# One set of work orders for another in a causal-attention kernel on one core, with two score banks and four transpose banks in PSUM where there were three and three

## What is computed (the reference, cut)

```python
h = layernorm(x) * (1 + ca) + sa                 # ca, sa, ga, ... come from silu(c) @ wmod, six sections
k, q, v = (einsum('ihd,bpd->biph', W, h) for W in (W_K, W_Q, W_V))
scores = einsum('biph,biqh->biqp', k, q)         # 2048 x 2048 for each head, causal mask
attn = softmax(masked / sqrt(128), axis=-1)
z = einsum('biqp,biph->biqh', attn, v)
x = x + ga * einsum('df,bqf->bqd', W_O, z_flat)
h = layernorm(x) * (1 + cb) + sb
w_gu, w_down = dequant_fp4(...)                  # packed 4-bit codes times group scales
y = einsum('bsi,hi->bsh', silu(gate) * up, w_down)   # gate, up = h @ w_gu
x = x + gb * y / rms(y)
```

## Time and profile before

| | us |
|---|---|
| three runs | 2268.33, 2266.88, 2264.04 (median 2266.88) |
| the profiled execution | 2263.7, with a span of 2261.9 |
| TensorE busy | 2124.0 of the span |
| VectorE, ScalarE, GpSimd busy | 1347.8, 1040.4, 714.0 |
| mean granted TensorE clock | 0.975 of full speed |

### The profile page before, as it was taken

How to read it: one execution, slowest core, us unless ns; L and a number is a source line. 1 busy time by engine, 2 the same in 40 slices (tenths; PEclk the granted TensorE clock), 3 DMA queues, 4 the chain that set the end, 5 groups by cost and what they waited for, 6 DMA issues and landing times. The chain is left out here.

```text
span 2261.9 us, 36789 instructions
## 1 busy us (share of the span) xinstructions
PE 2124.0 (94%) x12049; PEld 1831.7 (81%) x12049; DVE 1347.8 (60%) x3062; ACT 1040.4 (46%) x1947; POOL 714.0 (32%) x542
## 2 busy tenths in 40 slices
PE   6999798989989898999989899999999899999899
PEld 4778687978878797888879799999999788788687
DVE  7322365555646556565655656556556577799865
ACT  3322344544445454454545455555555333588611
POOL 4310233251523326143342600000005444388400
PEclk8999999999999999999999999999999999999999
DMA  7576302122120311212021120210223666211111
GB/s 251 175 206 190 109 27 87 32 67 63 39 70 26 86 42 60 63 35 72 23 86 49 49 63 11 63 56 12 60 63 100 211 233 200 106 59 38 52 65 65
DMA packets 171419, 189.99 MB, mean 84 GB/s; under 512 B 13395, under 2 KB 119123, under 8 KB 171219
## 3 DMA queue, kind: packets, MB, share of 16 engines
q1 hardware_dynamic: 169043, 184.89, 26.4%
q10 hardware_dynamic: 2304, 4.20, 0.5%
HBM read 121.53 MB, written 67.50 MB: 84 GB/s over the span
## 5 line engine op out<-in xcount | busy, mean ns | idle before, releaser
L1055 ACT ACTIVATE pT_hi<-ps_t 128x512 fp32r<-128x512 f32 (+3 forms) x640 | 303.5, 535 | 255.5 <-PE ps_t L993 253.2
L1063 ACT ACTIVATE probs<-probs,rmin 128x128 f32<-128x128 f32 (+15 forms) x256 | 309.1, 1207 | 196.3 <-DVE rmin L1127 195.8
L1136 DVE TENSOR_TENSOR pT_lo<-ps_t,pT_hi 128x512 fp32r<-128x512 f32 (+3 forms) x640 | 355.8, 603 | 61.7 <-ACT pT_hi L1055 58.7
L192 PE MATMUL ps_z<-pT_hi,v_hi 128*128 128x256 f32 (+1 forms) x1152 | 324.5, 282 | 27.1 <-DVE pT_lo L1136 27.1
L193 PE MATMUL ps_z<-pT_lo,v_hi 128*128 128x256 f32 (+1 forms) x1152 | 328.0, 285 | 0.0
L194 PE MATMUL ps_z<-pT_hi,v_lo 128*128 128x256 f32 (+1 forms) x1152 | 327.4, 284 | 0.0
L192 PE MATMUL ps_s<-kT_hi,qT_hi 128*128 128x512 f32 (+3 forms) x640 | 251.2, 392 | 51.9 <-DVE rmin L1127 27.7
L993 PE MATMUL ps_t<-ident,probs 128*128 128x128 f32 x2176 | 282.9, 273 | 4.3 <-ACT probs L1063 4.3
L993 PEld LDWEIGHTS ps_t<-ident,probs 128*128 128x128 f32 x2176 | 248.6, 141 | 19.9 <-ACT probs L1063 4.9
L192 PEld LDWEIGHTS ps_z<-pT_hi,v_hi 128*128 128x128 f32 x1152 | 223.2, 194 | 37.8 <-issue 31.8
L194 PE MATMUL ps_s<-kT_hi,qT_lo 128*128 128x512 f32 (+3 forms) x640 | 237.6, 371 | 0.0
(11 more groups left out here) (148 smaller groups left out, 4251.2 us busy)
## 6 DMA issues: line engine op xcount, KB each, us to landing
scratch_v<-p_vo_hi SPq DMA_DIRECT2D x64, 256.0 KB, 2.6
scratch_v<-p_vo_lo SPq DMA_DIRECT2D x64, 256.0 KB, 3.3
v_hi<-scratch_v SPq DMA_DIRECT2D x64, 256.0 KB, 3.8
v_lo<-scratch_v SPq DMA_DIRECT2D x64, 256.0 KB, 4.7
scratch_zT<-z SPq DMA_DIRECT2D x256, 64.0 KB, 1.7
w_raw<-in_w_qkv SPq DMA_DIRECT2D x16, 512.0 KB, 6.1
o_z<-scratch_zT SPq DMA_DIRECT2D x16, 512.0 KB, 6.6
o_scales<-scratch_recips SPq DMA_DIRECT2D x16, 512.0 KB, 7.6
```

The lines of the kernel that those rows point to most:

```text
L192: nc.tensor.matmul(dst, stat[0], mov[0], start=start, stop=False)
L1055: nc.scalar.activation(pT[0][:, slot, i % 2, 0:w], ps_t[:, (chunks_before(i) + u) % T_BANKS, 0:w], ACT.Copy).then_inc(t_hi, 1)
L1063: nc.scalar.activation(probs[:, i % 2, 0:w], probs[:, i % 2, 0:w], ACT.Exp, bias=rmin[:, i % 2:i % 2 + 1], scale=-1.0, accum_out=sums[:, i ...
L1136: nc.vector.tensor_tensor(pT[1][:, slot, i % 2, 0:w], ps_t[:, (chunks_before(i) + u) % T_BANKS, 0:w], pT[0][:, slot, i % 2, 0:w].bitcast(F ...
```

## The change

The three orders of the attention and the five of the prologue are replaced by others with the same words, `S_BANKS` goes from 3 to 2 and `T_BANKS` from 3 to 4 (six PSUM banks as before), and SyncE loads no v ahead of `w_raw` and the words of piece 0, except in head 0. The diff, with the ScalarE orders and the GpSimd order of the prologue left out:

```diff
--- before.py
+++ after.py
@@ -72,25 +72,26 @@
 
 
 PE_ORDER = """
-    S0.0 S1.0 S2.0 T15.0- T15.1- T15.2- PQ1.0 PQ1.1 PQ1.2 PQ1.3 Z7.0- Z7.1- T15.3- Z7.2- S3.0 Z7.3- N0- T0.0 T1.0
-    PK2.0 PK2.1 PK2.2 PK2.3 T2.0 S4.0 Z0.0 S4.1 PQ2.0 PQ2.1 PQ2.2 PQ2.3 T3.0 T4.0 T4.1 S5.0 S5.1 S6.0 Z1.0 PK3.0 S6.1
-    S7.0 S7.1 T5.0 T5.1 PK3.1 S8.0 S8.1 Z2.0 Z2.1 T6.0 T6.1 T7.0 S8.2 PK3.2 S9.0 T7.1 PK3.3 Z3.0 Z3.1 S9.1 S9.2 T8.0
-    T8.1 T8.2 S10.0 S10.1 PQ3.0 PQ3.1 PQ3.2 PQ3.3 S10.2 T9.0 T9.1 T9.2 S11.0 S11.1 S11.2 Z4.0 Z4.1 Z4.2 T10.0 T10.1
-    T10.2 S12.0 S12.1 S12.2 T11.0 T11.1 T11.2 PQ0.0+ S12.3 PQ0.1+ S13.0 Z5.0 Z5.1 Z5.2 S13.1 S13.2 S13.3 T12.0 T12.1
-    T12.2 S14.0 S14.1 T12.3 S14.2 PQ0.2+ PQ0.3+ S14.3 T13.0 T13.1 T13.2 S15.0 S15.1 PK0.0+ PK0.1+ PK0.2+ PK0.3+ Z6.0
-    Z6.1 T13.3 T14.0 T14.1 Z6.2 Z6.3 S15.2 S15.3 T14.2 T14.3 PK1.0+ PK1.1+ PK1.2+ PK1.3+
+    S0.0 PK1.0 PK1.1 T15.0- T15.1- T15.2- PK1.2 S1.0 PK1.3 Z7.0- Z7.1- PQ1.0 PQ1.1 PQ1.2 PQ1.3 T15.3- T0.0 Z7.2- S2.0
+    T1.0 S3.0 Z7.3- N0- T2.0 S4.0 S4.1 PK2.0 Z0.0 PK2.1 PK2.2 PK2.3 T3.0 T4.0 T4.1 S5.0 S5.1 PQ2.0 PQ2.1 PQ2.2 PQ2.3
+    Z1.0 S6.0 S6.1 T5.0 T5.1 PK3.0 S7.0 S7.1 Z2.0 Z2.1 T6.0 T6.1 S8.0 S8.1 T7.0 T7.1 S8.2 PK3.1 PK3.2 Z3.0 S9.0 Z3.1
+    S9.1 S9.2 PK3.3 T8.0 T8.1 T8.2 S10.0 S10.1 PQ3.0 PQ3.1 PQ3.2 PQ3.3 S10.2 T9.0 T9.1 T9.2 S11.0 S11.1 Z4.0 T10.0
+    T10.1 T10.2 Z4.1 S11.2 Z4.2 PQ0.0+ S12.0 PQ0.1+ S12.1 S12.2 T11.0 T11.1 T11.2 S12.3 S13.0 Z5.0 Z5.1 S13.1 S13.2
+    Z5.2 S13.3 T12.0 T12.1 T12.2 T12.3 S14.0 S14.1 PQ0.2+ S14.2 S14.3 T13.0 T13.1 T13.2 T13.3 PQ0.3+ S15.0 Z6.0 Z6.1
+    S15.1 PK0.0+ PK0.1+ PK0.2+ S15.2 S15.3 PK0.3+ Z6.2 Z6.3 T14.0 T14.1 T14.2 T14.3
 """
...
 DVE_ORDER = """
-    C0.0 UK1 L15.0- L15.1- L15.2- UQ1 C1.0 L15.3- C2.0 X0 L0.0 L1.0 C3.0 UK2 L2.0 C4.0 C4.1 UQ2 L3.0 L4.0 L4.1 C5.0
-    C5.1 C6.0 X1 C6.1 C7.0 L5.0 L5.1 C7.1 C8.0 L6.0 L6.1 L7.0 C8.1 L7.1 C8.2 C9.0 X2 C9.1 C9.2 UK3 L8.0 L8.1 L8.2
-    C10.0 C10.1 C10.2 UQ3 L9.0 L9.1 L9.2 C11.0 C11.1 C11.2 L10.0 L10.1 L10.2 C12.0 C12.1 L11.0 L11.1 L11.2 C12.2 C12.3
-    C13.0 C13.1 C13.2 C13.3 L12.0 L12.1 L12.2 C14.0 C14.1 L12.3 C14.2 C14.3 UQ0+ L13.0 L13.1 L13.2 UK0+ C15.0 L13.3
-    L14.0 L14.1 C15.1 C15.2 C15.3 L14.2 L14.3 R0
+    C0.0 L15.0- L15.1- L15.2- UK1 C1.0 UQ1 L15.3- L0.0 C2.0 L1.0 C3.0 X0 C4.0 L2.0 C4.1 UK2 L3.0 L4.0 L4.1 C5.0 C5.1
+    UQ2 C6.0 C6.1 L5.0 C7.0 L5.1 C7.1 X1 C8.0 L6.0 L6.1 L7.0 L7.1 C8.1 C8.2 C9.0 C9.1 C9.2 UK3 C10.0 C10.1 L8.0 L8.1
+    L8.2 C10.2 UQ3 L9.0 X2 L9.1 L9.2 C11.0 L10.0 L10.1 L10.2 C11.1 C11.2 C12.0 C12.1 C12.2 L11.0 L11.1 L11.2 C12.3
+    C13.0 C13.1 C13.2 C13.3 L12.0 C14.0 C14.1 L12.1 L12.2 L12.3 C14.2 L13.0 L13.1 L13.2 L13.3 C14.3 C15.0 UQ0+ C15.1
+    C15.2 C15.3 UK0+ R0 L14.0 L14.1 L14.2 L14.3
 """
 
 
@@ -136,8 +137,8 @@
 SPLITS = 2 * len(MATS)
 PIECES = 3
 PT_SLOTS = 5
-S_BANKS = 3
-T_BANKS = 3
+S_BANKS = 2
+T_BANKS = 4
 
 
 def pair_chunks(b):
@@ -400,15 +401,15 @@
 
 
 
-    PE_FIRST = """M0 M1 T0.0 T0.1 T0.2 T0.3 T1.0 T1.1 V0 V1 M2 T1.2 T1.3 V2 V3 T2.0 V4 T2.1 T2.2 T2.3 V5 V6 V7 V8 V9
-        V10 T3.0 T3.1 T3.2 V11 T3.3 M3 V12 V13 V14 M4 M5 V15"""
...
-    DVE_FIRST = """S0 G0 N0 G1 S1 L0.0 L0.1 L0.2 N1 L0.3 S2 S3 X0 L1.0 X1 G2 N2 X2 X3 L2.0 X4 N3 X5 X6 X7 X8 X9 X10 L3.0
-        X11 G3 X12 X13 X14 G4 G5 X15"""
...
-    SP_FIRST = """Rc Rm0 Rx0 Rm1 Rv0 Rx1 Rx2 Rx3 Rw Rm2 Rm3 Rv1 O0 O1 Rm4 O2 O3 O4 Rv2 O5 O6 O7 O8 O9 O10 O11 Rm5 O12
-        O13 O14 O15"""
+    PE_FIRST = """M0 M1 T0.0 T0.1 T0.2 T0.3 V0 V1 T1.0 T1.1 T1.2 T1.3 V2 V3 M2 V4 V5 T2.0 T2.1 T2.2 T2.3 V6 V7 M3 V8 V9
+        T3.0 T3.1 T3.2 T3.3 V10 V11 M4 V12 V13 M5 V14 V15"""
...
+    DVE_FIRST = """S0 G0 N0 G1 S1 L0.0 L0.1 L0.2 L0.3 N1 X0 X1 S2 L1.0 L1.1 X2 N2 X3 G2 S3 X4 X5 L2.0 L2.1 N3 X6 X7 G3 X8
+        X9 L3.0 L3.1 X10 X11 G4 X12 X13 G5 X14 X15"""
...
+    SP_FIRST = """Rc Rm0 Rx0 Rm1 Rv0 Rx1 Rx2 Rx3 Rm2 Rm3 Rv1 O0 O1 O2 O3 Rm4 O4 O5 Rv2 Rw O6 O7 Rm5 O8 O9 O10 O11 O12 O13
+        O14 O15"""
     V_FIRST = NT
 
     def entries(text):
@@ -816,8 +817,9 @@
             sp.dma_start(w_raw[:, n % 3, :], w_o[:, n, :]).then_inc(wo_loaded[n % 3], 16)
 
         def head(h, decode, first, last):
-            for u in range(NB if first else 2):
-                load_v(h, u)
+            if first:
+                for u in range(NB):
+                    load_v(h, u)
             if last:
                 sp.wait_ge(w_split, SPLITS * H)
                 for n in range(3):
@@ -830,7 +832,7 @@
                 load_piece(h, 0)
             if not first:
                 save_z(h - 1, NPAIR - 2)
-                for u in range(2, NB):
+                for u in range(NB):
                     load_v(h, u)
                 save_last_z(h - 1)
             if decode:
```

More of the change, by code:

```diff
@@ L82 @@
+    S9.1 S9.2 PK3.3 T8.0 T8.1 T8.2 S10.0 S10.1 PQ3.0 PQ3.1 PQ3.2 PQ3.3 S10.2 T9.0 T9.1 T9.2 S11.0 S11.1 Z4.0 T10.0
+    T10.1 T10.2 Z4.1 S11.2 Z4.2 PQ0.0+ S12.0 PQ0.1+ S12.1 S12.2 T11.0 T11.1 T11.2 S12.3 S13.0 Z5.0 Z5.1 S13.1 S13.2
+    Z5.2 S13.3 T12.0 T12.1 T12.2 T12.3 S14.0 S14.1 PQ0.2+ S14.2 S14.3 T13.0 T13.1 T13.2 T13.3 PQ0.3+ S15.0 Z6.0 Z6.1
+    S15.1 PK0.0+ PK0.1+ PK0.2+ S15.2 S15.3 PK0.3+ Z6.2 Z6.3 T14.0 T14.1 T14.2 T14.3
 """
 ACT_ORDER = """
-    E0 H15.0- H15.1- H15.2- UQ1 H15.3- E1 G0- Y7- H0.0 H1.0 E2 UK2 H2.0 E3 Y0 E4 UQ2 H3.0 H4.0 H4.1 Y1 E5 H5.0 H5.1 E6
@@ L85 @@
-    E7 Y2 H6.0 H6.1 H7.0 H7.1 UK3 E8 Y3 H8.0 H8.1 H8.2 E9 UQ3 H9.0 H9.1 H9.2 E10 E11 Y4 H10.0 H10.1 H10.2 H11.0 H11.1
-    H11.2 E12 Y5 H12.0 H12.1 H12.2 E13 H12.3 UQ0+ H13.0 H13.1 H13.2 E14 UK0+ H13.3 H14.0 H14.1 Y6 H14.2 H14.3 E15 UK1+
+    E0 H15.2- UK1 UQ1 H15.3- E1 H0.0 H1.0 E2 E3 G0- Y7- H2.0 Y0 E4 UK2 H3.0 H4.0 H4.1 E5 UQ2 Y1 H5.0 E6 H5.1 E7 Y2
+    H6.0 H6.1 H7.0 H7.1 E8 Y3 UK3 E9 H8.0 H8.1 H8.2 UQ3 H9.0 E10 H9.1 H9.2 H10.0 H10.1 H10.2 Y4 E11 H11.0 H11.1 H11.2
+    E12 Y5 H12.0 E13 H12.1 H12.2 H12.3 H13.0 H13.1 H13.2 H13.3 UQ0+ E14 UK0+ E15 Y6 H14.0 H14.1 H14.2 H14.3 H15.0
@@ L87 @@
+    H15.1
 """
 DVE_ORDER = """
-    C0.0 UK1 L15.0- L15.1- L15.2- UQ1 C1.0 L15.3- C2.0 X0 L0.0 L1.0 C3.0 UK2 L2.0 C4.0 C4.1 UQ2 L3.0 L4.0 L4.1 C5.0
-    C5.1 C6.0 X1 C6.1 C7.0 L5.0 L5.1 C7.1 C8.0 L6.0 L6.1 L7.0 C8.1 L7.1 C8.2 C9.0 X2 C9.1 C9.2 UK3 L8.0 L8.1 L8.2
-    C10.0 C10.1 C10.2 UQ3 L9.0 L9.1 L9.2 C11.0 C11.1 C11.2 L10.0 L10.1 L10.2 C12.0 C12.1 L11.0 L11.1 L11.2 C12.2 C12.3
-    C13.0 C13.1 C13.2 C13.3 L12.0 L12.1 L12.2 C14.0 C14.1 L12.3 C14.2 C14.3 UQ0+ L13.0 L13.1 L13.2 UK0+ C15.0 L13.3
@@ L398, in prologue @@
     rows_kept = {2: gate_a, 5: gate_b}
-    PE_FIRST = """M0 M1 T0.0 T0.1 T0.2 T0.3 T1.0 T1.1 V0 V1 M2 T1.2 T1.3 V2 V3 T2.0 V4 T2.1 T2.2 T2.3 V5 V6 V7 V8 V9
-        V10 T3.0 T3.1 T3.2 V11 T3.3 M3 V12 V13 V14 M4 M5 V15"""
-    ACT_FIRST = """D0 H0 H1 H2 H3 A0.0 A0.1 A0.2 D1 A0.3 A1.0 A1.1 D2 Y0 Y1 D3 A1.2 A1.3 Y2 Y3 A2.0 Y4 A2.1 A2.2 A2.3
-        Y5 Y6 Y7 Y8 Y9 Y10 A3.0 A3.1 A3.2 Y11 A3.3 Y12 Y13 Y14 Y15"""
-    DVE_FIRST = """S0 G0 N0 G1 S1 L0.0 L0.1 L0.2 N1 L0.3 S2 S3 X0 L1.0 X1 G2 N2 X2 X3 L2.0 X4 N3 X5 X6 X7 X8 X9 X10 L3.0
-        X11 G3 X12 X13 X14 G4 G5 X15"""
-    POOL_FIRST = """I0 I1 I2 I3 WK WQ L1.1 J1.0 J1.1 L1.2 L1.3 J1.2 J1.3 L2.1 L2.2 L2.3 L3.1 L3.2 L3.3"""
-    SP_FIRST = """Rc Rm0 Rx0 Rm1 Rv0 Rx1 Rx2 Rx3 Rw Rm2 Rm3 Rv1 O0 O1 Rm4 O2 O3 O4 Rv2 O5 O6 O7 O8 O9 O10 O11 Rm5 O12
-        O13 O14 O15"""
+    PE_FIRST = """M0 M1 T0.0 T0.1 T0.2 T0.3 V0 V1 T1.0 T1.1 T1.2 T1.3 V2 V3 M2 V4 V5 T2.0 T2.1 T2.2 T2.3 V6 V7 M3 V8 V9
+        T3.0 T3.1 T3.2 T3.3 V10 V11 M4 V12 V13 M5 V14 V15"""
+    ACT_FIRST = """D0 H0 H1 H2 H3 A0.0 A0.1 A0.2 D1 A0.3 Y0 Y1 A1.0 A1.1 A1.2 D2 A1.3 Y2 Y3 Y4 D3 Y5 A2.0 A2.1 A2.2 A2.3
+        Y6 Y7 Y8 Y9 A3.0 A3.1 A3.2 A3.3 Y10 Y11 Y12 Y13 Y14 Y15"""
+    DVE_FIRST = """S0 G0 N0 G1 S1 L0.0 L0.1 L0.2 L0.3 N1 X0 X1 S2 L1.0 L1.1 X2 N2 X3 G2 S3 X4 X5 L2.0 L2.1 N3 X6 X7 G3 X8
+        X9 L3.0 L3.1 X10 X11 G4 X12 X13 G5 X14 X15"""
+    POOL_FIRST = """I0 I1 I2 I3 L1.2 L1.3 J1.0 J1.1 J1.2 J1.3 L2.2 L2.3 L3.2 L3.3 WK WQ"""
+    SP_FIRST = """Rc Rm0 Rx0 Rm1 Rv0 Rx1 Rx2 Rx3 Rm2 Rm3 Rv1 O0 O1 O2 O3 Rm4 O4 O5 Rv2 Rw O6 O7 Rm5 O8 O9 O10 O11 O12 O13
+        O14 O15"""
     V_FIRST = NT
```

## The result

The changed kernel takes 2129.07 us (median; 2126.82 to 2129.75), the kernel before 2267.13 us beside it (2264.04 to 2268.33). The ratio is 0.9391, with a 95% interval of 0.9375 to 0.9408. The forecast was 2137 us, with 2122 to 2176.

The account below looks back on a forecast made before the run. TensorE bounds the kernel, losing 11.8 us per decoding head, with waits for late packed words and slowed clock. Savings 113 (heads 1 to 10) + 6 + 10 + 1 = 130 us from 2263.7, plus 3.2 for the median: 2137 us, range 2122 to 2176.

Parts of the forecast that it names:

- The floor and the 11.8 us: Attention heads: 86.8 us is a head's floor; the 11.8 us above it in heads 1 to 10 belong to decoding.
- The chain of 16.2 us: From X 0 to X 1, through GpSimd's piece, its save and the next words' load: 16.2 us; X 1 to X 2 16.3.
- the margin: At X 1 behind C 7.1: 16.7 us of TensorE work against 16.2, 0.5 us spare; words 1.9 us late stay hidden.
- X 0: First unpacking of a decoding head: with v no longer ahead in SyncE's queue, words get 25 us cover and no wait remains.
- The banks: Two score banks, four transpose banks: no wait found; 0.5 us a head allowed in heads 1 to 10, bounds 0 and 1.5.
- it buys no time where TensorE is full: Fourth transpose bank: lets T 13.1 and T 15 run ahead of L, but gains no time.
- Rival 3: Second score bank is the bound: score chunks wait for evictions; 8.1 us a head would undo the gain; chance 0.04.
- The rule that groups should rotate through banks: Score banks: skill's rule read as against the change, since two banks leave one chunk less lead and chunks would wait.
- Prologue and head 0: Prologue: V 0 and V 1 ahead of T 1 save 10 us (4 to 13); head 0 saves 6 (3 to 9).
- The last head: Behind the last head, TensorE's 2.72 us wait for tile 15's exponentials: 1 us saved, between -2 and 3.
- The median: Whole kernel: median of the runs taken as 3.2 us above the profiled execution's 2133.7, giving 2137.
- Rival 2: One X wait of three stays: 3.9 us in 11 heads, 43 us, giving 2180 us; chance 0.17.

Follow-up runs that it names:

- b_both: Kernel before, with only v no longer ahead of piece 0's words in SyncE's queue and X 0, X 1, X 2 moved later in VectorE's order: 2148.66 us, ratio 0.9465.
- b_queue: Kernel before, with only SyncE's queue changed (no v loads ahead of the words of piece 0): 2230.81 us, ratio 0.9829.
- a_x1_early: Changed kernel with X 1 moved forward, from behind C 7.1 to behind C 6.0: 2184.95 us, ratio 0.9632 to the kernel before.
- a_queue_back: Changed kernel with SyncE's queue as before, v of Z 7.0 and Z 7.1 ahead of the words: 2129.94 us, ratio 0.9385 to the kernel before.
- b_banks: Kernel before with two score banks and four transpose banks, nothing else: 2403.84 us, ratio 1.0591.
- a_score1: Changed kernel with one score bank and four transpose banks: 2631.47 us, ratio 1.1604 to the kernel before.
- a_banks33: Changed kernel with three score and three transpose banks: 2218.78 us, ratio 0.9781 to the kernel before.
- b_unpack_late: Kernel before with only X 0, X 1 and X 2 moved to their later places, queue as before: 2181.25 us, ratio 0.9610.

## Why the prediction was right, point by point

**The floor and the 11.8 us.** Right. Decoding heads are at 86.7 us, the floor taken from heads 11 to 14. That the words and not the rest of the decoding made the difference was argued from the earlier trace rows; b_both shows it, and so does the view of stretches after, where the same GpSimd and VectorE work costs TensorE nothing. One wait of head 10 was overlooked, a fourth of 0.31 us at a projection (1280.93); the waits are 7.1 us of the 12.9 and not 6.8, which changes nothing in the sum.

**The chain of 16.2 us.** Right, and the best supported number: where X 1 waited for its words it was 16.21 in b_queue, 16.18 in a_x1_early, 16.19 in a_queue_back and 16.26 in b_both. In the changed kernel 16.71 us lie between, so the margin is the 0.5 of the prediction. The count of TensorE's work was right to a tenth for X 1 (16.7), and 0.35 too low for X 2 (18.2 against 18.55).

**X 0.** Its cover is there (the words are issued 31 us ahead of it, and landing took 6.7 before the change), but it wasn't needed: a_queue_back shows that 1.84 us of wait at X 0 costs nothing in the new order. The prediction gave the queue's edit a part in the result that it has only in the old order (38 us).

**The banks.** The sum was right in what it led to, and one of its sentences was wrong. Two score banks cost nothing (no score chunk of heads 1 to 14 waits): the 0.5 us a head, 5 us in all, allowed for them was not needed, and by itself it covers the 4 us between the forecast span of 2131.9 (2133.7 less 1.8) and the measured 2128.0; head 0 gave 1.3 us less than forecast. But "it buys no time where TensorE is full", said of the fourth transpose bank, falls: without it the same order is 90 us slower. The step that failed took the transposes' lead over L for a luxury; I had worked out the margins of T with four banks and not what three would have done, and overlooked T 0.0. The banks are no gain by themselves (b_banks loses 135 us); they are a condition of the order.

**Rival 3** (the score banks as the bound) did not come in the new order. In the old one it would have: b_banks loses 135 us, 8.4 a head, where the rival needed 8.1. The rule that groups should rotate through banks (the Trainium skill, Perfetto Trace Analysis, section Matmuls) is borne out by a_score1, where nothing rotates. It says nothing of how many banks an order needs, so it did not speak against two, as the prediction had it: in b_banks and in the changed kernel chunks rotate through two banks alike, and only the first loses.

**Prologue and head 0.** 10.6 and 4.7 us against 10 and 6; of the waits forecast for head 0, 1.4 us at PQ1 and as much at T 2.0, the first is there with 1.41, and T 1.0 and T 2.0 wait 0.54 and 0.58. **The last head** saved 0.6 us against 1; the small waits shown above stand at its end, and whether the two banks cause them was not tried by itself.

**The median.** The 3.2 us added for it were not there: the changed kernel's profiled execution (2129.75) is 0.7 above its median. With the 4 us above, that makes the 8 us by which the forecast was high.

**Rival 2** did not come: no X 1 waited in any of the 11 heads, and a_queue_back shows that 1.2 us of lateness would still have been hidden. Its price for one stall, 3.9 us a head, was too low (5.2 by the head of a_x1_early).

## What to carry to other kernels

Where several engines follow fixed lists, a wait for a transfer belongs where the chain behind the transfer has run: measure the chain once (here 16.2 us from one unpacking to the next), count the work of the bounding engine between the two places, and move the word until it is longer. Compare iterations with and without the side work to get the floor. And take buffer counts together with the order they were made for: each of these two orders lost 4 to 6% with the other's banks, so a count tried on an unchanged order says little about the count.

## What the runs showed of the hardware that was not expected

A short gap on TensorE costs more than itself. In a_banks33 five waits of 4.0 us cost 5.6 us a head, with the clock at 1.00 in the whole stretch: 0.2 to 0.3 us more than each wait, and 0.6 at one. The first 512-column matmul behind such a wait lasts 0.50 us by its modelled end and not 0.39, as in the earlier trace rows. What comes on top is the clock, and the same wait can cost it or not. Heads 11 and 12 of b_banks have the same orders and, but for 0.1 us, the same eleven waits (7.55 and 7.67 us); the first loses 10.8 us at a clock of 1.00, the second 12.5 at 0.98. They part behind one wait of 1.03 us. The first two matmuls behind it, in head 11 and in head 12:

```profile
1444.57 0.50 PE L192 MATMUL ps_s<-kT_hi,qT_hi 128*128 128x512 f32 x1 [1.03 <-DVE probs L1123]
1444.90 0.39 PE L193 MATMUL ps_s<-kT_lo,qT_hi 128*128 128x512 f32 x1
...
1542.27 0.69 PE L192 MATMUL ps_s<-kT_hi,qT_hi 128*128 128x512 f32 x1 [1.03 <-DVE probs L1123]
1542.75 0.63 PE L193 MATMUL ps_s<-kT_lo,qT_hi 128*128 128x512 f32 x1
```

In the same way the granted clock fell to 0.50 (1.2 GHz) for 6.7 us behind the 2.95 us of the earlier trace rows, and matmuls of 0.63 us followed the wait of 2.0 in b_unpack_late, while the 1.98 us at T 0.0 in a_banks33 left the clock at 1.00. What decides between the two was not measured.
